# Scores of two heads issued together in the even slots, with the set-up loads and two set-up steps put elsewhere

## The reference

```
x = L0(x)   # down to 64, gelu, a 64x64 expert of the sample's domain, up to 256, + x, LayerNorm, gain and offset
x = L1(x)   # LayerNorm(x)*(1+scale)+shift from the sample's timestep; 16 heads of 16:
            #   probs = softmax(q k^T / 4 + side[b, h], masked);  x1 + ctx @ Wo;  then
            #   x2 + W2 . gelu(W1 . LN(x2)), with 1024 hidden columns
x = L2(x)   # one of three small networks by the sample's kind, + x, LayerNorm, gain and offset
x = L3(x)   # max(f + dt*(second and first differences along both axes of f times five fixed grids), 0)
```

## Time and profile before

| | |
|---|---|
| time, median of 3 runs | 876.44 us (875.49 to 876.72) |
| the profiled execution | 875.6 us |
| its span | 873.7 us |
| busy PE, DVE, ACT, POOL | 810.6, 738.0, 621.9, 164.5 us |
| mean granted clock of TensorE | 0.97 |
| read from HBM | 98.23 MB |

### The profile page before, as it was taken

How to read it: one execution, slowest core, us unless ns; L and a number is a source line. 1 busy time by engine, 2 the same in 40 slices (tenths; PEclk the granted TensorE clock), 3 DMA queues, 4 the chain that set the end, 5 groups by cost and what they waited for, 6 DMA issues and landing times.

```text
span 873.7 us, 18591 instructions
## 1 busy us (share of the span) xinstructions
PE 810.6 (93%) x5968; PEld 693.5 (79%) x5968; DVE 738.0 (84%) x2474; ACT 621.9 (71%) x1284; POOL 164.5 (19%) x160
## 2 busy tenths in 40 slices
PE   5593899999999999999999999999999999999992
PEld 2472578888888888888888898888888888887782
DVE  4744776898989989898989899898989899878787
ACT  2433767887978787887878787878879787677541
POOL 3210102212220303021122203021222212111020
PEclk9967999999999999999999999999999999999996
DMA  5467578577685867576577857576766757574100
GB/s 175 130 191 215 128 182 186 144 181 179 156 194 139 185 151 187 156 173 163 166 180 173 174 153 177 150 194 148 185 161 154 193 146 174 137 177 127 50 31 24
DMA packets 147593, 137.33 MB, mean 157 GB/s; under 512 B 19282, under 2 KB 144787, under 8 KB 147492
## 3 DMA queue, kind: packets, MB, share of 16 engines
q1 hardware_dynamic: 146532, 135.28, 62.2%
q10 hardware_dynamic: 960, 0.79, 0.5%
HBM read 98.23 MB, written 4.23 MB: 117 GB/s over the span
## 4 chain that ended last, share of the span: by engine, by line
PE 82%; DVE 9%; issue 4%; SPq 3%; ACT 1%; ACTq 1%; POOL 0%; DMA 0%; DVEq 0%; POOLq 0%
PE back_bank L1359 12%; PE turn_bank L1315 12%; PE context_bank L1369 7%; PE score_bank L1555 7%; PE score_bank L1556 6%; PE front_bank L1353 5%; PE attend_bank L1353 5%; PE back_bank L1353 5%; PE front_bank L1408 3%; PE back_bank L1339 3%; PE back_bank L1330 3%; PE attend_bank L1339 3%; PE front_bank L1661 2%; PE attend_bank L1300 2%; PE attend_bank L1377 2%
## 5 line engine op out<-in xcount | busy, mean ns | idle before, releaser
L560 ACT ACTIVATE sc<-sc,negmax 128x256 f32<-128x256 f32 x512 | 231.2, 504 | 26.2 <-DVE negmax L1191 25.4
L1191 DVE CUSTOM_DVE_ANT_0 sc<-score_bank,side 128x256 f32<-128x256 f32 x512 | 195.2, 418 | 50.5 <-PE score_bank L1556 34.4
L554 ACT ACTIVATE pt<-turn_bank 128x512 f32<-128x512 f32 x176 | 105.7, 601 | 136.2 <-PE turn_bank L1315 108.6
L1315 PE MATMUL turn_bank<-ident,sc 128*128 128x128 f32 x1024 | 156.4, 276 | 1.3 <-ACT sc L560 1.3
L1315 PEld LDWEIGHTS turn_bank<-ident,sc 128*128 128x128 f32 x1024 | 123.2, 141 | 31.8 <-issue 13.9
L1555 PE MATMUL score_bank<-ks,qs 128*128 128x256 f32 x512 | 123.4, 323 | 3.9 <-issue 3.8
L1359 PE MATMUL back_bank<-w,ffT 128*128 128x256 f32 x512 | 118.5, 379 | 0.4 <-DVE ffT L1100 0.4
L1359 PEld LDWEIGHTS back_bank<-w,ffT 128*128 128x128 f32 x512 | 96.8, 190 | 13.4 <-DVE ffT L1100 1.0
L480 POOL TENSOR_TENSOR rstd<-var,half_neg 128x2 f32<-128x2 f32 x64 | 50.8, 794 | 283.9 <-DVE var L953 282.4
L1556 PE MATMUL score_bank<-mask_neg,ident_r 128*128 128x512 f32 x256 | 102.6, 401 | 0.0
L1555 PEld LDWEIGHTS score_bank<-ks,qs 128*128 128x128 f32 x512 | 79.2, 194 | 12.0 <-issue 10.7
(11 more groups left out here) (246 smaller groups left out, 1956.3 us busy)
## 6 DMA issues: line engine op xcount, KB each, us to landing
side<-in_side SPq DMA_DIRECT2D x128, 512.0 KB, 5.2
qs<-qh SPq DMA_DIRECT2D x128, 64.0 KB, 4.1
qs<-ql SPq DMA_DIRECT2D x128, 64.0 KB, 4.2
ks<-kl SPq DMA_DIRECT2D x124, 64.0 KB, 4.1
ks<-kh SPq DMA_DIRECT2D x120, 64.0 KB, 3.9
wb<-in_wb SPq DMA_DIRECT2D x15, 512.0 KB, 6.5
xN<-in_x SPq DMA_DIRECT2D x16, 256.0 KB, 4.4
wc<-in_wc SPq DMA_DIRECT2D x16, 256.0 KB, 2.8
```

Of the source, the lines that this page charges most:

```text
L554: e.activation(pt[:, h % NP2, :, :], two(tbank[h % 2]), ACT.Copy).then_inc(copied[h % 4], 1)
L560: i = e.activation(sc[:, h % NS, q, :], sc[:, h % NS, q, :], ACT.Exp, bias=negmax[:, q, h:h + 1], scale=-1.0)
L1191: i = e.tensor_tensor_reduce(sc[:, s % NS, q, :], two(sbank[s % 2])[:, q, :], side[:, (H * X.i + s) % NSIDE, q, :], -1.0, 3.4e38, ALU.add, ...
L1315: i = e.transpose(tbank[h % 2][:, k * S + q * P:k * S + q * P + P], sc[:, h % NS, q, k * P:k * P + P], ident[:, :])
```

## The change

- **Scores in pairs.** The three matmuls of a score become a function, and in even slots it is called for heads s and s+1, one after the other; odd slots have none. Each still waits for `biased` of the head two before it, so the score of head s+1 waits for head s-1.
- **Order inside two odd slots.** In slot 3 the flips go ahead of `differ(U, 1)`, in slot 11 ahead of the feed-forward quarter.
- **Loads.** Grids, difference matrices and the three rows are issued in slot 1 of turn -1; w2 in two halves in slots 7 and 11 of turn 0, wa in slot 15. The counts on `ld_late` go from 7 to 8 (and 8 to 9).
- **Set-up steps.** ScalarE's scaling of w2 goes from slot 8 of turn 0 to slot 5 of turn 1; VectorE's `set_derivatives` from slot 14 of turn 0 to slot 9 of turn 1; ScalarE's eight packing DMAs of turn 0 from ahead of `vp` to behind it.

```
-            def load_rest():
-                load(ld_late, (w2[:, :, :], blocks(d["w2"])))
+            def load_grids():
                 load(ld_grid, (t_a[:, :, :], tall(d["grid_B"][0])), (t_b[:, :, :], tall(d["grid_B"][1])), (t_c[:, :, :], tall(d["grid_B"][2])),
                      (x2[:, :, :], tall(d["grid_A"][0])), (x3[:, :, :], tall(d["grid_A"][1])))
-                load(ld_late, (wa[:, :, :], blocks(d["wa"])), (t_u[:, :, :], blocks(d["d1T"])), (t_r2[:, :, :], blocks(d["d2T"])),
+                load(ld_late, (t_u[:, :, :], blocks(d["d1T"])), (t_r2[:, :, :], blocks(d["d2T"])),
                      (b2r[:, :], d["b2"].partition_broadcast(P)), (gamma3[:, :], d["gamma3"].partition_broadcast(P)),
                      (beta3[:, :], d["beta3"].partition_broadcast(P)))
+            def load_w2(n):
+                ks_ = slice(FM // 2 * n, FM // 2 * n + FM // 2)
+                load(ld_late, (w2[:, ks_, :], blocks(d["w2"])[:, ks_, :]))
+            def load_wa():
+                load(ld_late, (wa[:, :, :], blocks(d["wa"])))
+            later = {(-1, 1): load_grids, (0, 7): lambda: load_w2(0), (0, 11): lambda: load_w2(1), (0, 15): load_wa}
...
-                    if is_step(t, s, 0, 1):
-                        load_rest()
+                    if (t, s) in later:
+                        later[t, s]()
...
-                    if is_step(t, s, 0, 8):
-                        e.wait_ge(ld_late, 7 * 16)
+                    if is_step(t, s, 1, 5):
+                        e.wait_ge(ld_late, 8 * 16)
                         e.activation(w2[:, :, :], w2[:, :, :], ACT.Copy, scale=0.5).then_inc(act_set, 1)
...
                     if s == 9 and F:
...
                         e.activation(vp[:, F.par, :, :, 0:DH], two(fbank).rearrange("p t (h c) -> p t h c", h=H), ACT.Copy).then_inc(ev["v_ready"], 1)
+                        if t == 0:
+                            e.wait_ge(ev["kl_ready"], F.n)
+                            e.wait_ge(ev["kh_ready"], F.n)
+                            head(e, scored, X, HM - 1)
+                            for b in range(NBLK):
+                                for u in range(2):
+                                    pack_k(e, 0, b, u)
...
-                                          (0, 12, set_edges), (0, 14, set_derivatives)):
+                                          (0, 12, set_edges), (1, 9, set_derivatives)):
...
+            def score(x, h):
+                head(e, biased, x, h - 2)
+                for q in range(TT):
+                    e.matmul(two(sbank[h % 2])[:, q, :], qs[:, h // 2, q * P:q * P + P], ks[:, h, :], start=(q == 0), stop=False)
+                i = e.matmul(sbank[h % 2][:, :], ident_r[:, :], mask_neg[:, x.par, :, :], start=False, stop=True)
+                i.then_inc(scored[h % 4], 1)
...
-                    if X:
+                    if X and s % 2 == 0:
...
+                        score(X, s)
+                        score(X, s + 1)
...
                             turn(bbank, x3, ev["x3_turned"])
+                        four(flip)
                         if U:
                             differ(U, 1)
-                            four(flip)
...
                     elif s == 11:
+                        for n in range(4):
+                            flip(n)
                         if B:
...
                             project_T_parts(bbank, w1, w1l, 0, n3h, n3l, 2, ev["w1_done"])
-                        for n in range(4):
-                            flip(n)
```

More of the change, by code:

```diff
@@ L715, in body @@
                                     pack_k(e, 0, b, u)
+                    if s == 9 and F:
+                        e.wait_ge(ev["v_done"], F.n)
+                        wait(e, ev["mixed"], 4 * (F.i - 1))
+                        if t == -1:
+                            e.wait_ge(pool_set, VP_SET)
+                        e.activation(vp[:, F.par, :, :, 0:DH], two(fbank).rearrange("p t (h c) -> p t h c", h=H), ACT.Copy).then_inc(ev["v_ready"], 1)
                         if t == 0:
@@ L722, in body @@
                                     pack_k(e, 0, b, u)
[L723 to L728, removed]
                     if s == 10 and G and t != -1:
@@ L1497, in last_turns @@
                 e.wait_ge(ld_kind, times(T, 32) - 16)
-                e.wait_ge(ld_late, 8 * 16)
+                e.wait_ge(ld_late, 9 * 16)
                 condition(T, kind, wb_last)
@@ L1545, in body @@
                     if is_step(t, s, 2, 5):
-                        e.wait_ge(ld_late, 7 * 16)
-                    if X:
+                        e.wait_ge(ld_late, 8 * 16)
+                    if X and s % 2 == 0:
                         if s % HM == 0:
                             e.wait_ge(ld_stack[s // HM], times(X, STACKED))
-                        head(e, biased, X, s - 2)
                         if s == 0:
                             e.wait_ge(ev["mask_ready"], X.n)
[L1554 to L1557, removed]
+                        score(X, s)
+                        score(X, s + 1)
                     flip = no_more
@@ L1590, in body @@
                             turn(bbank, x3, ev["x3_turned"])
+                        four(flip)
                         if U:
                             differ(U, 1)
-                            four(flip)
-                        else:
-                            for n in range(4):
-                                flip(n)
                     elif s == 4:
```

## The result

The changed kernel takes 894.19 us (median of four runs, 893.47 to 894.66), the kernel before 876.58 us beside it (875.49 to 877.38): ratio 1.0201, 95% interval 1.0183 to 1.0219, so it is 2.0% slower. The profiled execution has a span of 891.7 us against 873.7 us.

The account below looks back on a forecast made before the run. TensorE was taken to set the pace, with VectorE and ScalarE nearly as full for a third of each turn. Start -11.2 and later turns +20.9 gave +9.7 on 875.6: 885.3, with 0.8 for the median 886 us; range 873 to 892.

Parts of the forecast that it names:

- 12 x 1.5 = +18.0: Turns 2 to 13: each loses 1.5 us as slot 0's second score waits for head 15; together +18.0.
- about 0.7 later: Turn 0: slot 2's pair waits for head 1, making x1 and the query projection about 0.7 us later.
- turn 14's +0.8: Turn 14 has no xN, but the score of head 1 of turn 15 comes too early: +0.8, between 0.6 and 1.1.
- Slot 9, vp: Value projection ends 0.47 us later, `vp` starts with it, no slack: xN transposes +0.47 on TensorE.
- Slot 10, n3: Second score adds another 0.47 us before n3's transposes; n3h and n3l start 0.94 later, passed on through VectorE to head 15.
- rival that had the delay absorbed: Steady turns: the n3 delay is absorbed, only head 15's 0.6 us a turn remains; total 875; chance 0.15.
- the rival that only TensorE's work counts: Steady turns cost 0, stalls caught up within the turn, the start's gain stays; total 865; chance 0.10.
- Turn 15, +1.6: Slot 14's pair waits 2.3 us for head 13, 0.5 comes back in slot 15: +1.6, between 0 and 2.5.
- Turn 0, -12.4: Earlier side load and full-clock key projection -11.1, packing -0.6, `set_derivatives` -0.7: together -12.4 us.
- Packing, -0.6: Turn 0: packing DMAs behind `vp` shift TensorE's wait one slot, from xN to `pt` and `xT`: -0.6, between 0 and -2.
- `set_derivatives`, -0.7: Two casts of 0.8 us leave slot 14 of turn 0, where VectorE sets the pace: -0.7.
- Turn 1, +1.7: w2's scaling in slot 5 plus pairs waiting in slots 2 and 4, +1.2, and the `vp` wait, +0.5.

Follow-up runs that it names:

- one pair undone: Changed kernel with score 9 issued in slot 9 again, all other pairs kept: 887.66 us, ratio 1.0121, period down by 0.53.
- slot 10 is undone: Changed kernel with score 11 issued in slot 11 again, all other pairs kept: 889.49 us, ratio 1.0143, period down by 0.49.
- with all three: Changed kernel with the scores of slots 0, 8 and 10 each in their own slot again, other pairs kept: 873.56 us, ratio 0.9953.
- undoing slot 0: Changed kernel with score 1 issued in slot 1 again, all other pairs kept: 886.24 us, ratio 1.0107, period down by 0.66.
- the run with the old order: Changed kernel, pairs kept, with the flips of slots 3 and 11 back in their earlier order: 892.51 us, ratio 1.0173.
- turn 0 single: Changed kernel with each score in its own slot in turn 0 only, pairs from turn 1 on: 892.94 us, ratio 1.0190.
- the kernel with w2 late: The single scores kernel with w2's scaling moved from slot 5 to behind kh in slot 8 of turn 1: 866.52 us, ratio 0.9879.
- single scores: Changed kernel with each score in its own slot and slots 3 and 11 in old order; loads and set-up as changed: 868.96 us, ratio 0.9915.
- the pairs by themselves: Kernel before with the scores in pairs and slots 3 and 11 reordered, nothing else: 904.02 us, ratio 1.0314.

## Why the prediction missed

The direction and the mechanism of the steady turns held; the time is outside the range. 9.7 us were forecast on the profiled execution and 17.9 came. The step that failed is the size of "12 x 1.5 = +18.0" for turns 2 to 13, which measured +21.9; turn 0's query projection, "about 0.7 later", and turn 14's +0.8 were too small as well. By the prediction's own steps:

- **Slot 9, vp: +0.47.** Held. Against score 0, xN's turn comes 1.25 us later than before (31.46 against 30.21), 0.76 of it from slots 0 to 7 and 0.49 from here; one pair undone gives 0.53 back.
- **Slot 10, n3: another +0.47, and the n3 delay passes through n3h and n3l whole.** Held: VectorE idle 0.80 before n3l (forecast 0.8), and 0.49 back when slot 10 is undone. The rival that had the delay absorbed is refuted by that run, and the rival that only TensorE's work counts by all of them. The prediction took a rule of the Trainium skill ("Perfetto Trace Analysis", "Identifying the Most-Contended Engine") to lead to the latter, reading TensorE's 93% as the highest occupancy. That section takes matmul busy time out of the comparison and judges TensorE by MFU (arithmetic done as a share of the peak) and the busy share of its weight loads, 79% of the span here, less than VectorE's 84%, so it doesn't point at TensorE alone. The trace shows what occupancy over the span leaves out: neither engine got work, and the turn 1.76 us.
- **"12 x 1.5", the steady part.** The 1.5 was already a sum of three delays: 0.6 of waiting for head 15 and twice 0.47 ahead of n3. All three held (0.57, 0.49 and 0.48 in turn 7) and they add, as the runs with one pair undone and with all three show. What failed is what the prediction put at nothing beside them. The first score after a wait costs 0.11 us more: undoing slot 0 gives 0.66 back, not 0.57. And the flips ahead of `differ` cost 0.08 by TensorE's rows and 0.14 by the run with the old order; the prediction named them for its upper bound of 1.8 and took 0. 0.57 + 0.11 + 0.08 + 0.49 + 0.48 = 1.73, the difference of turn 7. Over turns 3 to 13 the quarter of a microsecond makes 2.7 us.
- **Turn 2 taken as one of the twelve.** It measured 2.75 up to score 0 of turn 3, 1.25 more. It has no output stage yet, VectorE has less to do and TensorE paced it (46.48 against 48.37). Where a steady turn loses 0.76 in slots 0 to 7, turn 2 loses 1.77: no wait in slot 0 (score 1 stands 0.55 behind score 0), but score 5 waits 1.54 us for head 3, and 1.07 of it come from one VectorE instruction that runs longer beside GpSimd's.
- **Turn 14, +0.8.** Measured +2.3, and by another way. The wait forecast, of score 1 of turn 15 for its head, didn't come: it starts 0.55 behind score 0. At score 0 plus 33.97 us, against 32.97 before, n3's turn is 1.0 late: 0.6 from the wait and the order of its own slots 0 to 3, which the prediction counts to turn 13, the rest from slot 10's second score, which it left out here. Then the second score of slot 14 waits for head 13. Slots 12 and 14:

```profile
775.97 0.50 PE L1413 MATMUL score_bank<-ks,qs 128*128 128x256 f32 x2 [0.26 <-DVE negmax L1198]
781.84 0.51 PE L1413 MATMUL score_bank<-ks,qs 128*128 128x256 f32 x2 [0.95 <-DVE negmax L1198]
```

- **Turn 15, +1.6.** Measured +1.3, near it partly by luck: the second score of slot 14 waited 0.94 us, not 2.3, and that of slot 10, not forecast, 1.47. In the other kernels that pair slot 2 the end took 103.9 to 107.0 us (last section).
- **Turn 0, -12.4.** Measured -10.6. The wait for the side load went as said. "About 0.7 later in the end" for x1 and the query projection was the mis-sized term: the projection starts 2.3 us later (63.07 against 60.77). The pairs have 1.2 of it (61.87 with turn 0 single); 1.0 is there without pairs too (61.77 in the kernel with w2 late), with half clock lasting to 60.3 us instead of 57.5. In the single-score execution that had full clock earlier it starts at 59.29.
- **Packing, -0.6, and `set_derivatives`, -0.7.** Not separated by a run; the wait moved to slot 10 as said, 3.72 us long.
- **Turn 1, +1.7.** Measured +2.9. With single scores the turn is 3.0 longer than before, 2.4 of it from the scaling in slot 5 (forecast at most 2.5, taken 1.2); the pairs by themselves cost 1.5. In the changed kernel moving the scaling gave only 0.64 back, in an execution with a late packing DMA, so how the 2.9 divide isn't settled.

The whole start, turns 0 and 1, gained 7.7 us instead of 10.7; of the 8.2 us missed, 3.0 lie there, 2.7 in the steady turns and 2.75 in turns 2 and 14, and 0.3 the other way at the end.

## What to carry to other kernels

Delays in series along one cycle between engines add: undone one at a time, three pairs gave 1.68 us a turn back, undone together 1.66. Undoing one part at a time shows this to a few hundredths of a microsecond, since a periodic kernel gives the period and not only a total. A term with a bound of its own that is then put at nothing comes back once for each turn, so price it from its rows too. The turns at the two ends of a pipeline, where stages are missing, have other waits than the steady ones and want rows of their own. And price a set-up step by what stands behind it on its engine in that slot, then again by the clock that TensorE may lose if it idles there.

## What the runs showed of the hardware

The granted clock in the first heads isn't the same from kernel to kernel, and probably not from run to run. With single scores full clock came back at 48.5 us, at the start of b1's one-column matmuls; in the kernel before it stayed at 0.50 there, though TensorE was busy without a gap too. Single scores, then before, then the changed kernel:

```profile
48.00:50.00 2.00, 2.00 (x19) 2.00 (x17) 1.93 (x11) 1.27 (x3) 0.07 (x1) 0.88 0.27 94
50.00:52.00 2.00, 2.00 (x19) 2.00 (x20) 1.78 (x7) 1.03 (x3) 0.63 (x1) 0.98 0.29 101
```

```profile
48.00:50.00 2.00, 2.00 (x12) 2.00 (x11) 1.93 (x12) 1.39 (x3) 0.26 (x1) 0.50 0.31 107
58.00:60.00 2.00, 1.89 (x15) 1.49 (x13) 1.76 (x12) 2.00 (x6) 1.33 (x1) 1.00 0.95 287
```

```profile
48.00:50.00 2.00, 1.83 (x7) 1.65 (x8) 1.93 (x11) 0.91 (x2) 0.66 (x1) 0.50 0.31 102
58.00:60.00 2.00, 2.00 (x10) 1.72 (x9) 1.25 (x8) 1.25 (x3) 0.66 (x1) 0.50 1.06 332
```

With the same work up to there, single scores' turn 0 took 44.61 us and, with only a later step moved, 46.89. The 32 one-column matmuls for b1 are where they part. Single scores, then the same with w2 late:

```profile
48.22 3.77 PE L1554 MATMUL back_bank<-cols,ffT 128*128 128x1 f32 x32
```

```profile
48.15 6.83 PE L1554 MATMUL back_bank<-cols,ffT 128*128 128x1 f32 x32
```

That the clock makes the spread of the unprofiled runs (5.3 us with single scores) is argued, not shown.

The last turns have two causes of spread. In five of the nine kernels that pair slot 2 in all of these turns, turn 15 and the end took 103.9 to 104.5 us. In the other four an `edge_t` instruction of VectorE took 1.3 us beside one of GpSimd that had started before it, where it takes 0.17 elsewhere, and the end took 105.5 us in one and 106.3 to 107.0 in the three where half clock was granted for 3.4 us as well (with slot 10 single the stretch 813 to 829 us ran at 0.89, where the changed kernel had 1.00). So a difference of 2 to 3 us outside the steady turns can come from the clock and from such meetings of two engines, and only the periods of turns 3 to 13, which agree within a kernel to 0.1 us but for a few, are exact.
